# A recurrent agent on one core: other places for the history products, input products from fp16 parts, a later tanh

## The reference, cut to what matters

```python
encoded = tanh(xt @ We + st @ Ue + be)                       # 24 features
new_state = tanh(xt . Wx + st . Ws + bk)                     # 8 candidates of 32
inp = concat([encoded, err])                                 # 25 features
mem = concat([inp, mem[:-1]])                                # the last 20 steps
a = relu(mem.reshape(b, -1) @ enc_w1 + enc_b1)               # 500 -> 64
agent_in = relu(a @ enc_w2 + enc_b2)
h1, c1 = lstm_cell(agent_in, h1, c1, ...)
h2, c2 = lstm_cell(h1, h2, c2, ...)
gate = softmax(h2 @ gate_w + gate_b)
theta = clamp01(mean(abs(mem[:, :10, -1])) * 2.5)
gate = gate * theta + gs * (1 - theta)
st = sum over candidates of gate * new_state
pred = clamp01(st[:, -1]);  err = pred - yt
```

## Time and profile before

| | |
|---|---|
| median of 3 runs | 5403.86 us (5403.62 to 5405.82) |
| the profiled execution | 5403.15 us, its span 5401.2 us |
| TensorE matmuls busy | 5265.2 us, 97% of the span |
| VectorE busy | 4268.4 us, 79% |
| ScalarE busy | 4082.6 us, 76% |
| GpSimd busy | 2539.0 us, 47% |
| mean granted TensorE clock | 0.998 of full speed |

### The profile page before, as it was taken

The page is one execution under the profiler, slowest core; times in us unless marked ns, Lnnn a source line. Parts: engine busy times, 40 slices in busy tenths (PEclk is TensorE's granted clock), DMA queues, the critical chain, the costliest instruction groups (busy, mean ns, idle before and its releaser), DMA issues.

```text
span 5401.2 us, 184110 instructions
## 1 busy us (share of the span) xinstructions
PE 5265.2 (97%) x64512; PEld 3168.2 (59%) x64512; DVE 4268.4 (79%) x11822; ACT 4082.6 (76%) x10241; POOL 2539.0 (47%) x5125
## 2 busy tenths in 40 slices
PE   8999999999999999999999999999999999999998
PEld 4555555555555555555555555555555555555554
DVE  7777777777777777777777777777777777777777
ACT  5777777777777777777777777777777777777776
POOL 3444444444444444444444444444444444444444
PEclk9999999999999999999999999999999999999999
DMA  2111111111111111111111111111111111111111
GB/s 68 30 30 32 29 32 29 32 29 32 29 33 29 32 30 30 32 29 32 29 32 29 32 29 32 30 32 30 30 32 30 32 29 32 29 32 29 32 30 41
DMA packets 299271, 172.29 MB, mean 32 GB/s; under 512 B 156598, under 2 KB 263866, under 8 KB 298698
## 3 DMA queue, kind: packets, MB, share of 16 engines
q1 hardware_dynamic: 293560, 159.45, 11.8%
q10 hardware_dynamic: 5138, 3.53, 0.2%
HBM read 74.55 MB, written 2.10 MB: 14 GB/s over the span
## 4 chain that ended last, share of the span: by engine, by line
PE 91%; ACT 7%; issue 1%; DVE 0%; DMA 0%; POOL 0%; POOLq 0%; SPq 0%; DVEq 0%; ACTq 0%
PE a_ps L373 21%; PE chain L412 20%; PE a_ps L384 8%; PE cand_ps L354 8%; PE cand_ps L345 8%; ACT a_sb L516 7%; PE chain L317 6%; PE chain L324 6%; PE a_ps L395 4%; PE chain L290 3%; PE cand_ps L337 3%; PE cand_ps L302 3%; PE chain L429 1%; PE chain L422 0%; DMA cand<-in_bk 0%
## 5 line engine op out<-in xcount | busy, mean ns | idle before, releaser
L373 PE MATMUL a_ps<-hist,w_hist 125*64 125x512 f16 x12288 | 1889.6, 384 | 23.5 <-DMA w_hist<-enc_table 23.2
L807 DVE TENSOR_REDUCE state<-mixed 128x64 f32<-128x512 f32 x2048 | 1353.2, 682 | 34.2 <-POOL mixed L906 0.8
L906 POOL TENSOR_TENSOR mixed<-cand,gate 128x512 f32<-128x512 f32 x1024 | 1281.5, 1273 | 48.8 <-POOL gate L894 12.7
L535 ACT ACTIVATE cand<-cand_ps 128x512 f32<-128x512 f32 x2048 | 1103.1, 593 | 236.2 <-PE cand_ps L354 235.8
L412 PEld LDWEIGHTS chain<-cell_in,cell_w 128*64 128x64 f32 x16384 | 903.2, 136 | 406.5 <-ACT cell_in L524 248.6
L412 PE MATMUL chain<-cell_in,cell_w 128*64 128x128 f32 x16384 | 1120.5, 277 | 17.9 <-ACT cell_in L524 0.6
L373 PEld LDWEIGHTS a_ps<-hist,w_hist 125*64 125x64 f16 x12288 | 675.7, 110 | 494.5 <-issue 214.5
L872 POOL TENSOR_TENSOR one_theta<-ones,theta 128x8 f32<-128x8 f32 x512 | 103.1, 201 | 1563.1 <-DVE theta L684 1563.1
L549 ACT ACTIVATE gates<-chain 128x384 f32<-128x384 f32 x1024 | 502.3, 491 | 364.9 <-PE chain L412 362.2
L916 POOL COPY cell_in<-cell_in 128x256 f32<-128x256 f32 x512 | 202.8, 396 | 962.4 <-DVE cell_in L717 962.4
L542 ACT ACTIVATE chain<-cell_bias 128x512 f32<-128x512 f32 x1024 | 610.6, 596 | 16.1
(11 more groups left out here) (76 smaller groups left out, 7029.5 us busy)
## 6 DMA issues: line engine op xcount, KB each, us to landing
x_sb<-in_x_l SPq DMA_DIRECT2D x260, 256.0 KB, 2.8
hist<-entry_parts SPq DMA_DIRECT2D x2048, 25.0 KB
w_hist<-enc_table SPq DMA_DIRECT2D x258, 128.0 KB, 2.4
y_rows<-in_y_l SPq DMA_DIRECT2D x260, 8.0 KB
ys<-in_y ACTq DMA_DIRECT2D x1, 2048.0 KB, 16.4
preds_out<-preds SPq DMA_DIRECT2D x1, 2048.0 KB, 7.5
cand<-in_encoder ACTq DMA_DIRECT2D x1, 640.0 KB, 3.8
cell_w<-in_cell ACTq DMA_DIRECT2D x2, 256.0 KB, 5.1
```

The lines of the kernel that those rows point to most:

```text
L373: nc.tensor.matmul(a_ps[g][ENC * half:ENC * half + ENC, :], w_hist[0:HROWS, w_slot(u), kk, wp, :], hist[0:HROWS, xp, k, at:at + 512], star ...
L535: ins = nc.scalar.activation(cand[:, g, q // 2, :, q % 2, :, :].rearrange("p h s c -> p h (s c)"), cand_ps[q][:, :].rearrange("p (h k) -> ...
L807: V.tensor_reduce(state[:, g, hf, 2 * pair:2 * pair + 2, :], mixed[:, pair, hf, :, :, :], AX, ALU.add)\
L906: G.tensor_tensor(mixed[:, 0, :, q, :, :], cand[:, g, 0, :, q, :, :], over_s, ALU.mult)\
```

## The change

1. **History.** Before, tile 2 of `cur` was the first thing in TensorE's phase (two pairs, then one behind the state transposes), tile 0 of `new` and tile 3 of `cur` were spread between `encoded_s` and the encoder. Now two pairs of tile 2 are done a phase earlier, between the candidates and `encoded_x`; one pair is left ahead of the state transposes and none behind them; tile 3 stands in one piece behind `encoded_s`, none between the logits and `encoder1_now`; tile 0 follows it in one piece. The wait for the history's DMA and weights (`history_waits`) moves behind `encoder1_now`.
2. **Input's candidates' products.** `w_x` is split once, `x` in each phase into a high and a low fp16 part. GpSimd makes the parts (`x_high`, a copy; `x_low`, a subtraction) behind its two mixing operations and ahead of `next_hidden`, with a wait for the hidden state of `cur`. TensorE does 24 fp16 matmuls (three pieces, two halves, four quarters) with 256 columns each, where there were 8 fp32 products, which the profile shows as 16 matmuls.
3. **Candidates' order.** Quarters 2, 3, 1, then 0. Quarter 0's tanh is the last, behind the agent input's ReLU and ahead of `keep_hidden`. The prediction's strip moves from bank 0 to bank 2.
4. **VectorE.** `error_sum` comes ahead of `prediction`.

```diff
-CAND_ORDER = (3, 0, 1, 2)
+CAND_ORDER = (2, 3, 1, 0)
...
+        w_x_parts = sb("w_x_parts", [P, 2, NS], FP16)
...
+        x_parts = sb("x_parts", [P, GROUPS, 2, COLS], FP16)
...
             def prediction_transpose(item):
                 g, n, u = item
                 pe.wait_ge(q_pred, n)
-                pe.wait_ge(q_cand[0], n)
+                pe.wait_ge(q_cand[2], n)
                 for hf in range(HF):
-                    last = nc.tensor.matmul(cand_ps[0][0:Q, P * hf:P * hf + P],
+                    last = nc.tensor.matmul(cand_ps[2][0:Q, P * hf:P * hf + P],
...
             def candidates_x(item):
                 g, n, u = item
+                pe.wait_ge(q_xl, n)
                 for hf in range(HF):
-                    for q in range(Q):
-                        rows = slice(D_IN * q, D_IN * q + D_IN)
-                        nc.tensor.matmul(cand_ps[q][:, NS * hf:NS * hf + NS],
-                                         x_sb[rows, x_slot(u), g, P * hf:P * hf + P], w_x[rows, :],
-                                         start=False, stop=False, skip_group_check=True)
+                    for wp, xp in PIECES:
+                        for q in range(Q):
+                            rows = slice(D_IN * q, D_IN * q + D_IN)
+                            nc.tensor.matmul(cand_ps[q][:, NS * hf:NS * hf + NS],
+                                             x_parts[rows, g, xp, P * hf:P * hf + P], w_x_parts[rows, wp, :],
+                                             start=False, stop=False, skip_group_check=True)
...
             def phase(items, extra):
                 new, cur, old = items
                 if cur:
-                    history(cur, 2, 0, 2)
+                    history(cur, 2, 2, 3)
                     state_transpose(cur, 0)
                     state_transpose(cur, 1)
-                    history(cur, 2, 2, 3)
                     prediction_transpose(cur)
                     encoded_s(cur)
-                if new:
-                    history_waits(new, extra)
-                    history(new, 0, 0, 1)
-                if cur:
-                    history(cur, 3, 0, 2)
+                    history(cur, 3)
                 if old:
                     logit_bias(old)
                     gate_logits(old)
                 if cur:
-                    history(cur, 3, 2, 3)
                     encoder1_now(cur)
                 if new:
-                    history(new, 0, 1, 3)
+                    history_waits(new, extra)
+                    history(new, 0)
                     history(new, 1, 0, 1)
                 if cur:
                     encoder2(cur)
...
                     candidates_x(cur)
                     candidates_s(cur)
                 if new:
+                    history(new, 2, 0, 2)
                     encoded_x(new, extra)
                 if cur:
                     cell_gates(cur, 1)
...
                 if cur:
-                    candidates(cur, 0)
+                    candidates(cur, 3)
                     candidates(cur, 1)
                     cell_tanhs(cur, 1)
...
                 if cur:
-                    candidates(cur, 2)
                     exponentials(cur)
...
                     agent_input(new, 0)
                 if cur:
+                    candidates(cur, 0)
                     keep_hidden(cur)
...
                     value_tanh(new, 0)
-                    candidates(new, 3)
+                    candidates(new, 2)
...
+            link(V.tensor_copy(w_x_parts[:, 0, :], w_x[:, :]))
+            link(V.tensor_tensor(w_x_parts[:, 1, :], w_x[:, :], w_x_parts[:, 0, :], ALU.subtract))
...
+                if cur:
+                    error_sum(cur)
+                if old:
                     prediction(old)
                 if cur:
-                    error_sum(cur)
                     cell_terms(cur, 1)
...
+            def x_wait(item, extra):
+                g, n, u = item
+                if g == 0:
+                    pool.wait_ge(s_x[x_slot(u)], extra[3][u] if extra else 16)
+
+            def x_high(item, other):
+                g, n, u = item
+                pool.wait_ge(s_ready, 1)
+                if other:
+                    pool.wait_ge(q_h[0], n - 1)
+                G.tensor_copy(x_parts[:, g, 0, :], x_sb[:, x_slot(u), g, :]).then_inc(q_xh, 1)
+
+            def x_low(item):
+                g, n, u = item
+                pool.wait_ge(q_xh, n)
+                G.tensor_tensor(x_parts[:, g, 1, :], x_sb[:, x_slot(u), g, :], x_parts[:, g, 0, :],
+                                ALU.subtract).then_inc(q_xl, 1)
...
                 new, cur, old = items
+                if new:
+                    x_wait(new, extra)
                 if old:
                     gate_in_sbuf(old)
                     mix_quarter(old, 1)
                     mix_quarter(old, 0)
+                if new:
+                    x_high(new, cur)
+                    x_low(new)
+                if old:
                     next_hidden(old, cur)
```

More of the change, by code:

```diff
@@ L147, in recurrent_kernel @@
         q_in_high = sem("q_in_high")
+        q_xh, q_xl = sem("q_xh"), sem("q_xl")
         q_bias = [sem(f"q_bias{c}") for c in range(2)]
@@ L694, in errors @@
                 dve.wait_ge(q_predps, n)
-                V.tensor_tensor(entry[ZR:ER, g, :], cand_ps[0][0:Q, 0:COLS], y_rows[0:Q, x_slot(u), g, :],
+                V.tensor_tensor(entry[ZR:ER, g, :], cand_ps[2][0:Q, 0:COLS], y_rows[0:Q, x_slot(u), g, :],
                                 ALU.subtract)\
@@ L930, in place @@
                     return STEPS - 1, STEPS % WINDOW
-                step, odd, even = extra
+                step, odd, even, x_count = extra
                 after = u + 2
@@ L959, in turn_start @@
                 even = pool.snap((turn + 1) % 2 * PER_TILE)
-                return step, odd, even
+                x_count = [pool.snap(turn * 16 + 16)] * (PER_TILE - 1) + [pool.snap(turn * 16 + 32)]
+                return step, odd, even, x_count
             def phase(items, extra):
                 new, cur, old = items
+                if new:
+                    x_wait(new, extra)
                 if old:
```

## The result

The kernel after took 5342.14 us (median of 4 runs), the kernel before 5404.77 us in the same runs: ratio 0.9885, 95% interval 0.9873 to 0.9897. The direction was as forecast, but of the 194 us only 63 came, and the time lies above the stated range (5160 to 5300). The clamp's view says it by phase: (5329.0 - 50.6) / 511 = 10.33 us, where the kernel before had 10.45. The forecast's 10.05 is counted from TensorE's phase of 10.43 us; between clamps it means 10.45 - 0.38 = 10.07.

What follows compares the result with a forecast made beforehand. TensorE bounds the kernel (91% of the chain). Per phase -0.10 - 0.22 + 0.01 - 0.07 = -0.38 us, times 511 = 194 us; 5403.15 - 194 + 1 (start) = 5210 us, range 5160 to 5300.

Steps and rivals of the forecast that it cites:

- The shorter products: Input's candidates' products on TensorE as 24 fp16 matmuls: 0.65 us a phase instead of 0.86, 0.21 less.
- the new wait for the state copy: TensorE from L290 to L324: a new 0.24 us wait for ScalarE's copied state, so the stretch shrinks only 0.10 us.
- the stretch to the encoder: TensorE from L324 to L384: one history pair goes, 0.22 us less, 1.30 instead of 1.52.
- GpSimd's new pair: GpSimd's copy and subtraction for the input's parts, behind the hidden state: 1.1 to 1.3 us, costing nothing.
- no stall of the sums: VectorE's last sums end 4.81 us after the first L412, L290 comes at 4.99: ready by some 0.2 us.
- the ReLU's stretch: TensorE from L384 to L395: 1.83 us, 0.01 more, since ScalarE's ReLU covers the fourth history pair.
- the last stretch: TensorE from the first L412 to the next L290: 0.07 us less than 5.06, including the input products' 0.21.
- The step that failed: VectorE's hidden state, 3.50 us after the first L412, is ready before TensorE reaches the second L412 at 3.75.
- Two of the signs of being wrong: Listed signs: second L412 still led by the hidden state; a longer L702 (VectorE's cell terms) while GpSimd works.
- The rival that came near: GpSimd's new operations hold up VectorE's cell terms, giving back some 0.1 us a phase: 5261 us, chance 0.05.
- The second rival: Waits on state copy, tanh or ReLU eat the new order; only the shorter products' gain remains: 5297 us, chance 0.14.

## Why the prediction was wrong

**Steps that held.** The shorter products (0.65 us for 0.65), the new wait for the state copy (0.91 for 0.92, named by the trace), the stretch to the encoder (1.32 for 1.30), GpSimd's new pair behind the hidden state with nobody waiting for it, no stall of the sums (though they end only 0.03 us ahead of L293, at 13.75 + 1.28 = 15.03, and not 0.2). With the terms free, the run with half of quarter 0 left out has the forecast's time: 5211 for 5210 us. That it is so near is partly luck: in its timeline the ReLU's stretch takes 0.05 us a phase more than forecast and the last stretch 0.04 less, and with all the work done the best run needs 5230 us.

**The step that failed** is in the stretch from the first L412 to the next L290: "The hidden state ends 3.50 us after the first L412", taken from the kernel before and carried over. In the kernel after it is 13.72 - 9.84 = 3.88 us. Two of the signs of being wrong that it listed came true together: the second gate product still led by the hidden state, and longer terms while GpSimd works. The prediction moved the cell forward against the gate without laying out GpSimd's mixing against VectorE's cell terms in the new order. From the logits' bias (L422) to the first gate product it was 3.22 us before and is 3.07 after, since a history pair between the two is gone. From the same point to the mixing it was 2.48 us and is 2.74 after. GpSimd's order there is the same in both kernels, but the row of small operations that ends with the weighted exponentials begins when VectorE's theta is there: 0.12 us ahead of the logits' bias (9.56) in the kernel before, 0.13 behind it (6.77) in the kernel after. VectorE forms theta behind the second cell, and from the second gate product to the next logits' bias the new order of TensorE takes 6.77 + 10.33 - 13.82 = 3.28 us where it took 9.56 + 10.43 - 16.38 = 3.61.

```profile
3009.44 0.20 POOL L872 TENSOR_TENSOR one_theta<-ones,theta 128x8 f32<-128x8 f32 x1 [3.03 <-DVE theta L684]
```

```profile
3006.90 0.21 POOL L877 TENSOR_TENSOR one_theta<-ones,theta 128x8 f32<-128x8 f32 x1 [1.89 <-DVE theta L687]
```

So the weighted exponentials come 0.25 us later against the logits, and VectorE now waits 0.33 us for them. Together that is 0.41 us, and the mixing, which used to end 0.09 us after the terms began, ends 0.51 after.

**The rival that came near** was the third. It had the right mechanism and put it at the wrong place: "only the cell terms could be hit" meant the terms that follow GpSimd's new operations, at "some 0.1 us a phase". Those operations ended before the second cell's terms began (14.95 + 0.39 = 15.34 in GpSimd's timeline, against 15.47); the old mixing held up the first cell's, by 0.37 us (0.79 for 0.42). Of that TensorE felt 0.23: it was to come to the second gate product 3.75 us after the first, 0.25 behind the hidden state, and came 3.98 after it. By the Trainium skill (SBUF — State Buffer, section "Who interferes with whom") a VectorE instruction with two SBUF inputs and a GpSimd instruction that reads SBUF exclude each other for a whole instruction, whichever comes second waits, and a reduction never contends. The traces agree: the terms end a constant 0.28 us behind GpSimd's operation, GpSimd's subtraction is stretched in its turn (0.86 for 0.67), and the reductions keep their 0.68 to 0.69 us. The row I had set beside it, sums next to a copy, was one that the rule lets through, so it could not have shown the cost.

**What the range lacked.** The smaller misses (0.05 us at the ReLU, 0.02 at the encoder), whose cause stays open, would have stayed inside it. The second rival's 5297 us left the shorter products as the sure part of the gain. They were the part that was worth nothing as long as VectorE was late.

## What to carry to other kernels

When a change moves one chain forward against another, lay out every pair of engines that share something in the new order, not only the chain's own waits; an operation that "only just" misses another in the old trace is the first to look at. A shorter product ahead of a wait for another engine is worth nothing until that wait goes. Reordering 0.35 us of small operations on the idlest engine gave 111 us here, more than the whole change it mended, and with the old order of the tanhs it took 5230 us: both are faster than either kernel.

## What was unexpected of the hardware

The hold goes by the order of starting and has a fixed size: the held operation of VectorE ends its own length less some 0.14 us after GpSimd's. The terms (0.42 us alone) ended 0.27 to 0.28 us after the multiplication in four kernels, whether 0.26 or 0.51 us of it were still to run; the cell's value (0.29 alone) ended 0.14 us after the subtraction (5.11 + 0.64 against 4.75 + 0.86). Whether those 0.14 us lie at the end of GpSimd's printed time or at the start of VectorE's, no run decides. An operation of VectorE with one input in SBUF and one in PSUM (L792, 1.20 us in the kernel after, beside the mixing) was not held. Four fp16 row groups with 256 columns run at 0.65 / 6 = 0.108 us a round, so the loads of 93 ns a piece (the page's group of L350) stay hidden even where they fill most of a round.
